# Decoder layer on one core: residual rows ahead of the copies of V on the DMA queue, and cross attention in pairs of chunks

## The reference

```python
# cross attention, 16 heads of 64 (as the kernel computes it)
e   = clip(exp(q @ k.T / sqrt(64)), exp(-11), exp(11))
o   = (e @ v) / e.sum(-1)
x   = layernorm(x + concat(o) @ Wo + bo)
# each of 6 layers: local attention, window 32, rows of two tiles of 128 tokens
qkv = shift(x) @ Wqkv            # shift: half of the columns come from the row before
o   = softmax(mask(rot(l2norm(q)) @ rot(l2norm(k)).T * 8)) @ v
x1  = x + o @ Wo
x2  = x1 + ffn(layernorm(shift(x1)))
```

## Time and profile before

| what | value |
|---|---|
| median of three runs | 2269.71 us (2268.53 to 2270.89) |
| the profiled execution | 2269.04 us, span 2267.3 us |
| TensorE, matmuls | 2108.9 us busy, 93% |
| VectorE, ScalarE, GpSimd | 81%, 73%, 73% |
| mean granted TensorE clock | 0.984 of 2.4 GHz |
| cross attention | from about 325 us to 624 us |
| window layers | from 624 us to the end |

### The profile page before, as it was taken

How to read it: one execution, slowest core, us unless ns; L and a number is a source line. 1 busy time by engine, 2 the same in 40 slices (tenths; PEclk the granted TensorE clock), 3 DMA queues, 4 the chain that set the end, 5 groups by cost and what they waited for, 6 DMA issues and landing times. The chain is left out here.

```text
span 2267.3 us, 70752 instructions
## 1 busy us (share of the span) xinstructions
PE 2108.9 (93%) x26387; PEld 1429.3 (63%) x26387; DVE 1840.3 (81%) x2681; ACT 1662.4 (73%) x3300; POOL 1653.9 (73%) x1553
## 2 busy tenths in 40 slices
PE   5898769999979999999999999999999999999995
PEld 3555436666546676766667666666666666666674
DVE  4898957777788888888888888888888888888883
ACT  5888845454367788788788878878877787887773
POOL 4667843332378888888888888888888888888881
PEclk8999989999999999999999999999999999999997
DMA  2321220000023223222322322232232222223221
GB/s 76 110 65 64 65 73 2 1 1 1 1 52 78 70 60 79 69 71 67 82 71 56 83 69 70 69 77 76 56 83 70 70 69 73 77 59 83 70 64 47
DMA packets 103501, 140.43 MB, mean 62 GB/s; under 512 B 63376, under 2 KB 64400, under 8 KB 103056
## 3 DMA queue, kind: packets, MB, share of 16 engines
q1 hardware_dynamic: 103440, 139.64, 23.1%
HBM read 56.39 MB, written 1.31 MB: 25 GB/s over the span
## 5 line engine op out<-in xcount | busy, mean ns | idle before, releaser
L1727 PE MATMUL f_psA<-f_W,f_xT 128*128 (+1 forms) x1154 | 599.4, 615 | 8.9 <-ACT f_Vt L1479 3.6
L1617 DVE TENSOR_TENSOR f_m<-f_psA,f_tab 128x1024 f32<-128x1024 f32 x385 | 458.4, 1212 | 62.9 <-ACT f_sq L1461 62.9
L1397 POOL TENSOR_TENSOR f_qkr<-f_qkr,f_rn 128x1024 f32<-128x1024 f32 x192 | 361.2, 1902 | 17.2 <-POOL f_rn L1420 17.2
L1368 POOL TENSOR_TENSOR f_Pr<-f_Pr,f_rden 128x384 f32<-128x384 f32 x384 | 307.7, 833 | 74.4 <-DVE f_rden L1606 74.4
L1461 ACT ACTIVATE f_sq<-f_psA 128x512 f32<-128x512 f32 x385 | 222.0, 589 | 103.9 <-PE f_psA L1727 100.2
L1727 PEld LDWEIGHTS f_psA<-f_W,f_xT 128*128 128x128 f32 x1154 | 191.6, 189 | 129.5 <-issue 88.4
L1387 POOL TENSOR_TENSOR f_qkr<-f_m 128x512 f32<-128x512 f32 x192 | 243.6, 1269 | 18.9 <-DVE f_m L1617 18.9
L1388 POOL TENSOR_TENSOR f_qkr<-f_m 128x512 f32<-128x512 f32 x192 | 245.6, 1279 | 0.0
L794 POOL TENSOR_TENSOR x_Es<-x_E 128x512 f32<-128x512 f32 x64 | 81.0, 1266 | 205.9 <-DVE x_E L899 205.9
L1593 DVE TENSOR_REDUCE f_mx<-f_psS 128x8 f32<-128x768 f32 x192 | 183.4, 955 | 50.0 <-PE f_psS L1762 50.0
L1648 DVE TENSOR_REDUCE f_ssq<-f_sq 128x32 f32<-128x2048 f32 x96 | 218.5, 2276 | 0.0
(11 more groups left out here) (176 smaller groups left out, 4717.1 us busy)
## 6 DMA issues: line engine op xcount, KB each, us to landing
f_V<-f_Vt SPq DMA_DIRECT2D x96, 384.0 KB, 4.2
f_V<-f_Vt SPq DMA_DIRECT2D x96, 256.0 KB, 3.5
f_W<-in_f_W SPq DMA_DIRECT2D x48, 344.0 KB, 3.0
m_Cb<-m_BC_rows SPq DMA_DIRECT2D x64, 256.0 KB, 3.1
f_W<-in_f_W SPq DMA_DIRECT2D x48, 296.5 KB, 3.5
f_V<-f_Vt SPq DMA_DIRECT2D x48, 128.0 KB, 4.3
f_xsA<-xall SPq DMA_DIRECT2D x98, 32.0 KB
f_xsA<-xall SPq DMA_DIRECT2D x98, 31.8 KB
```

Of the source, the lines that this page charges most:

```text
L1368: pool.tensor_tensor(pv, pv, rv.unsqueeze(3).broadcast_to([P, 2, 2, KEYS]), ALU.mult).then_inc(Pr_ready[g][j], 1)
L1397: pool.tensor_tensor(qv, qv, rv.unsqueeze(3).broadcast_to([P, 2, GH, DH]), ALU.mult).then_inc(qkr_ready[g], 1)
L1617: dve.tensor_tensor(m12[:, j, :, half].rearrange("p m (h d) -> p m h d", d=DH), psA[n % 2][:, :].rearrange("p (h d) -> p h d", d=DH).unsqu ...
L1727: pe.matmul(psA[n % 2][:, :], xT[:, t, :], weights(i, W_QKV + n * 512, 512), start=True, stop=True).then_inc(A_full[n_fill], 1)
```

## The change

In the window layers SyncE waits for `x1_ready` and issues the `xsC` DMAs first, and only then the copies of V. In cross attention the loop goes over pairs of chunks: each stage is run for both chunks before the next one. `E` gets four buffers (`ES`) in place of two. `out_projection` is one call that takes both row tiles of a head pair together and waits for each pair's normalised output by itself; its results go to two fills, `wo0` and `wo1`. VectorE, ScalarE and the list `fills` follow the new order.

```diff
@@ cross_attention_block, TensorE
-            for g in range(CHUNKS + 1):
+            for g in range(0, CHUNKS + 1, 2):
                 b, c = divmod(g, NC)
-                if g + 1 < CHUNKS:
-                    project(g + 1)
                 if c == 2 and b >= 1:
-                    out_projection(b - 1, 1)
+                    out_projection(b - 1)
                 if g < CHUNKS:
                     scores(g)
+                    scores(g + 1)
...
-                if g >= 1:
+                if g >= 2:
+                    times_v(g - 2)
                     times_v(g - 1)
-                if c == 1 and b >= 1:
-                    out_projection(b - 1, 0)
-                if c == 3 and b + 1 < B:
+                if g + 2 < CHUNKS:
+                    project(g + 2)
+                    project(g + 3)
+                if c == 2 and b + 1 < B:
                     transpose_rows(b + 1)
                 if c >= 4 and b + 1 < B:
                     project_v(b + 1, c - 4)
+                    project_v(b + 1, c - 3)
-            def out_projection(b, t):
...
+            def out_projection(b):
+                places = [bank(b, f"wo{t}") for t in range(TPB)]
                 for c in range(NC):
+                    pe.wait_ge(O_free, b * NC + c + 1)
+                    for t in range(TPB):
+                        ps, full = places[t]
+                        ins = pe.matmul(ps[:, 0:D], OT[:, b % 2, c, t * P:(t + 1) * P], wo[:, c, :], start=(c == 0), stop=(c == NC - 1))
...
@@ cross_attention_block, VectorE
                 if g < CHUNKS:
                     clip(g)
-                if g >= 1:
+                if g >= 2:
+                    normalise(g - 2)
+                if g < CHUNKS:
+                    clip(g + 1)
+                if g >= 2:
                     normalise(g - 1)
...
@@ window_layers, SyncE, slot(i, t, stages)
                     shift_in(i + 1, t)
-
-                    u = i * 2 + t
-                    for j in range(2):
-                        sp.wait_ge(A_free[8 + j], u + 1)
-                        alone(sp, passed)
-
-                    at_least(sp, O_free[1], u - 1)
-                    sp.dma_start(V96[WIN:KEYS, t, 0, :], Vt[0:HQ, t, :]).then_inc(V96_ready[t], 16)
-                    sp.dma_start(V96[:, t, 1, :], Vt[WIN:P, t, :]).then_inc(V96_ready[t], 16)
-                    if t == 1:
-                        sp.dma_start(V96[0:WIN, 1, 0, :], Vt[P - WIN:P, 0, :]).then_inc(V96_ready[t], 16)
                 if "C" in stages:
                     sp.wait_ge(x1_ready, i * 2 + (t - 1))
...
+                if "A" in stages:
+
+                    u = i * 2 + t
+                    for j in range(2):
+                        sp.wait_ge(A_free[8 + j], u + 1)
+                        alone(sp, passed)
...
```

More of the change, by code:

```diff
@@ L693, in cross_attention_block @@
     CHUNKS = B * NC
+    ES = 4
     LO, HI = float(np.exp(-11.0)), float(np.exp(11.0))
@@ L748, in cross_attention_block @@
         block = ctx.enter_context(nc.Block())
-        fills = [(0, "cat"), (0, "qk0")]
-        for g in range(CHUNKS + 1):
+        fills = [(0, "cat"), (0, "qk0"), (0, "qk1")]
+        for g in range(0, CHUNKS + 1, 2):
             b, c = divmod(g, NC)
-            if g + 1 < CHUNKS:
-                fills.append(((g + 1) // NC, f"qk{(g + 1) % NC}"))
+            if c == 2 and b >= 1:
+                fills += [(b - 1, f"wo{t}") for t in range(TPB)]
             if g == 0:
                 fills += [(0, f"v{n}") for n in range(4)]
-            if c == 1 and b >= 1:
-                fills.append((b - 1, "wo"))
-            if c == 3 and b + 1 < B:
+            if g + 2 < CHUNKS:
+                fills += [((g + 2) // NC, f"qk{(g + 2) % NC}"), ((g + 3) // NC, f"qk{(g + 3) % NC}")]
+            if c == 2 and b + 1 < B:
                 fills.append((b + 1, "cat"))
             if c >= 4 and b + 1 < B:
-                fills.append((b + 1, f"v{c - 4}"))
-        fills.append((B - 1, "wo"))
+                fills += [(b + 1, f"v{c - 4}"), (b + 1, f"v{c - 3}")]
+        fills += [(B - 1, f"wo{t}") for t in range(TPB)]
         place = {f: (k % 2, k // 2) for k, f in enumerate(fills)}
@@ L841, in exponentials @@
                     act.wait_ge(S_full, 2 * g + j + 1)
-                    if j == 0 and g >= 2:
-                        act.wait_ge(O_full, g - 1)
-                    act.activation(E[:, g % 2, j, :, :], psS[(2 * g + j) % 4][:, :, :], ACT.Exp, scale=DH ** -0.5).then_inc(E_exp, 1)
+                    if j == 0 and g >= ES:
+                        act.wait_ge(O_full, g - ES + 1)
+                    act.activation(E[:, g % ES, j, :, :], psS[(2 * g + j) % 4][:, :, :], ACT.Exp, scale=DH ** -0.5).then_inc(E_exp, 1)
             def copy_qk(g):
@@ L856, in _ @@
             copy_qk(0)
-            for g in range(CHUNKS + 1):
+            copy_qk(1)
+            for g in range(0, CHUNKS + 1, 2):
                 b, c = divmod(g, NC)
-                if g + 1 < CHUNKS:
-                    copy_qk(g + 1)
                 if g < CHUNKS:
                     exponentials(g)
+                    exponentials(g + 1)
                 if g == 0:
@@ L865, in _ @@
                         evacuate_v(0, n)
-                if c == 1 and b + 1 < B:
+                if g + 2 < CHUNKS:
+                    copy_qk(g + 2)
+                    copy_qk(g + 3)
+                if c == 0 and b + 1 < B:
                     deviation(b + 1)
-                if c == 3 and b >= 1:
+                if c == 2 and b + 1 < B:
+                    scale_transposed(b + 1)
+                if c == 4 and b >= 1:
                     deviation2(b - 1)
-                if c == 3 and b + 1 < B:
-                    scale_transposed(b + 1)
                 if c >= 4 and b + 1 < B:
                     evacuate_v(b + 1, c - 4)
+                    evacuate_v(b + 1, c - 3)
             deviation2(B - 1)
@@ L906, in residual @@
             def residual(b):
-                ps, free = wait_fill(dve, b, "wo")
                 dve.wait_ge(res_ready, b + 1)
-                dve.tensor_tensor(res[:, :, :], res[:, :, :], ps[:, 0:TPB * D].rearrange("p (t d) -> p t d", d=D), ALU.add).then_inc(free, 1)
+                for t in range(TPB):
+                    ps, free = wait_fill(dve, b, f"wo{t}")
+                    dve.tensor_tensor(res[:, t, :], res[:, t, :], ps[:, 0:D], ALU.add).then_inc(free, 1)
             def moments2(b):
-                wait_evacuated(dve, b, "wo")
+                for t in range(TPB):
+                    wait_evacuated(dve, b, f"wo{t}")
                 layer_norm_stats(dve, passed, mom2_ready, chain, [res[:, j, :] for j in range(TPB)], stats2, mom2)
@@ L922, in _ @@
             hats(0)
-            for g in range(CHUNKS + 1):
+            for g in range(0, CHUNKS + 1, 2):
                 b, c = divmod(g, NC)
+                if c == 2 and b + 1 < B:
+                    hats(b + 1)
                 if c == 2 and b >= 1:
@@ L1002, in times_v @@
                 ins.then_inc(O_full, 1)
-            def out_projection(b, t):
[L1005 to L1010, removed]
-                for c in range(NC):
-                    ins = pe.matmul(ps[:, t * D:(t + 1) * D], OT[:, b % 2, c, t * P:(t + 1) * P], wo[:, c, :], start=(c == 0), stop=(c == NC - 1))
-                if t == TPB - 1:
-                    ins.then_inc(full, 1)
+            def out_projection(b):
+                places = [bank(b, f"wo{t}") for t in range(TPB)]
+                for c in range(NC):
+                    pe.wait_ge(O_free, b * NC + c + 1)
+                    for t in range(TPB):
+                        ps, full = places[t]
+                        ins = pe.matmul(ps[:, 0:D], OT[:, b % 2, c, t * P:(t + 1) * P], wo[:, c, :], start=(c == 0), stop=(c == NC - 1))
+                        if c == NC - 1:
+                            ins.then_inc(full, 1)
             transpose_rows(0)
             project(0)
-            for g in range(CHUNKS + 1):
+            project(1)
+            for g in range(0, CHUNKS + 1, 2):
                 b, c = divmod(g, NC)
-                if g + 1 < CHUNKS:
-                    project(g + 1)
                 if c == 2 and b >= 1:
-                    out_projection(b - 1, 1)
+                    out_projection(b - 1)
                 if g < CHUNKS:
                     scores(g)
+                    scores(g + 1)
                 if g == 0:
@@ L1036, in _ @@
                     project_v(b + 1, c - 4)
-            out_projection(B - 1, 0)
-            out_projection(B - 1, 1)
+                    project_v(b + 1, c - 3)
+            out_projection(B - 1)
 W_QKV = 0
@@ L1314, in slot @@
                     shift_in(i + 1, t)
+                if "C" in stages:
+                    sp.wait_ge(x1_ready, i * 2 + (t - 1))
+                    sp.dma_start(xsC[:, t, 0:64], x1[:, t, 0:64]).then_inc(xsC_ready[t], 16)
+                    sp.dma_start(xsC[1:P, t, 64:D], x1[0:P - 1, t, 64:D]).then_inc(xsC_ready[t], 16)
```

(3 more changed lines are left out.)

21 lines of the change are left out of this document (7 added, 14 removed).

## The result

The changed kernel takes **2354.28 us** (median of 4 runs, 2352.89 to 2357.59) against 2269.12 us for the kernel before in the same comparison: a ratio of 1.0376, 95% interval 1.0358 to 1.0394. It is slower, as forecast, but by 85 us and not 55, and 4 us beyond the upper end of my range. The profiled execution took 2353.36 us (span 2351.6).

A forecast was written before the change was run, and what follows sets the result against it. The prediction took TensorE's instruction list, 93% busy, as the bound. From the profiled 2269.04 us it summed -4 (cross attention), -13 (order's gain) and +74 (late V) to 2326, stated as 2325 us, range 2290 to 2350.

The forecast's parts named there:

- Direction and place: Whole kernel 2.4% slower, as ScalarE waits for V's late copies from t = 1 in the window layers; chance of slower 0.87.
- the wait, 1.6 taken: Window layers: ScalarE waits 1.6 us per iteration for V's copies, all lost on TensorE: +73.6 us.
- Case 2: Window layers: the engine busy with the 127-row DMA delays V in full, 2.0 us per iteration: 2344 us; chance 0.20.
- Case 5: Window layers: V's issues held back behind three small DMAs, 0.9 us on top of Case 2: 2385 us; chance 0.07.
- The gain of the order: Window layers, t = 0: earlier residual rows cut idle time before the second `scores` by 0.29 us per iteration: -13 us.
- Cross attention: -4 forecast: Cross attention in sum: -17.6 + 4 + 7.4 + 2 = -4 us, between -12 and +2.
- the 17.6: Cross attention: each of 32 chunk pairs pays 0.55 us for changes of the array's form once, not twice: -17.6 us.
- 4 and 7.4: Cross attention, seven batches: PSUM bank waits of 0.18 us three times each, +4; 1.05 us before each `out_projection`, +7.4.
- the last batch's gain: Cross attention, last batch, where no V is projected: VectorE is tight there, so its gain from pairing was given back.
- 2 for the start and the end: Cross attention: VectorE's later last normalise and four V fills at the start waiting for four exponentials: +2 us.
- Case 3: Window layers: V's copies land in time, within 6.1 us of the end of `x1`: faster, 2252 us; chance 0.11.
- Case 4: Window layers: TensorE's lost time covers other waits, 0.8 us less per iteration: 2289 us; chance 0.07.

The follow-up runs named there:

- experiments 2 and 3: The changed kernel with the new queue order at t = 0 only: ratio 0.9947; at t = 1 only: 1.0377; with four `Vt` buffers for two: 0.9923.
- one row: The changed kernel with the 127-row residual DMA L1329 cut to a single row, the others left zero: 2337.98 us, ratio 1.0287.
- experiment 5: Three variants of the changed kernel: single-row DMA L1331 behind V's copies, ratio 1.0349; 127-row DMA cut to 112 rows, 1.0297; to a single row, 1.0287.
- 112 rows: The changed kernel with the 127-row residual DMA L1329 cut to 112 rows, the last 15 left zero: 2340.95 us, ratio 1.0297.

## Why the prediction came out as it did

- **Direction and place: right.** V's copies became the late ones, at t = 1, 43 times in the stretch; experiments 2 and 3 show that this wait and nothing else makes the loss. That TensorE loses nearly the whole of it holds: 1.92 - 0.30 = 1.62, and the period grows by 1.51.
- **The failed step is the sum's form.** I priced TensorE's idle time at its own length, once per iteration. The runs show a second price: 13 iterations in which the granted clock falls to 1.2 GHz, 1.58 us each, 21 us in all. It was in no case and in no bound of the range. Without it the time would be 2353 - 21 = 2332 us, inside the range. I had read a full clock in the earlier trace rows and taken it as a constant, though it had been read where TensorE never waited longer than 0.64 us in an iteration.
- **A term mis-sized: the wait, 1.6 taken, 1.94 measured.** I had V's first issue 2.1 us behind the end of `x1`; it stands at 2.39. Between the end of L1331's issue (1589.48 + 0.87) and L1340 there are 0.27 us and not 0.04, where SyncE's list has its waits on V. The landing adds 0.1 (4.4 against 4.3). 1.5 + 0.29 + 0.1 = 1.9. With the gain taken off, an iteration was priced at 1.31 us and grew by 1.51, 9 us over 46; this error alone, without the drops, would have left the time inside the range, and so would the drops alone without it.
- **Case 2, right in size by another cause.** Its 2.0 us is nearly what was measured, but its mechanism is not. By the rule that I drew from the Trainium skill (DMA: Bandwidth & Descriptors, section "Queues, rings and completion order") one engine's ring would delay V by 0.5 us. With one row in place of 127 V's landing stays at 4.5 us. That doesn't refute the rule: L1329 is issued at 1588.81, its engine is free 3.2 us later, at 1592.0 by the earlier trace rows, and V's data starts to move 1.2 us behind 1590.62, at 1591.8, so hardly anything overlaps. The row that landed behind all of V in experiment 5 agrees with it.
- **Case 5, issue held back: didn't come.** V's three issues took 0.49, 0.59 and 0.59 us behind the small ones. What there is of it, 0.28 us in L1331's issue, was in the sum already, which had 0.86 for it.
- **The gain of the order: right where it can be seen.** 0.57 became 0.27 as forecast, so 0.3 per iteration, and the sum above needs it.
- **Cross attention: -4 forecast, -8 measured** (the kernel with the pairs alone is 7 us faster). Seven batches bring 7 x 0.82 = 5.7. My terms for them give 4.0 (15.4 of the 17.6, less 4 and 7.4): a pair with V takes 8.40 to 8.46 us and not 8.5, and the wait ahead of the output projection is 0.9 us and not 1.05. I had given the last batch's gain back and added 2 for the start and the end; they bring some 2.5 as well.
- **The weights of the cases.** Case 3 (faster) decided at 6.1 us from the end of `x1` to the landing; it took 3.56 + 4.4 = 8.0. Case 4 (half absorbed) had nothing for it in any run.

## What to carry to other kernels

A queue that is issued in order is a schedule: before a DMA is moved ahead, ask of each one that it passes how much slack it has, and where a buffer is given back late, count a second buffer before a second order. Here two more buffers turned 3.8% slower into 0.8% faster. Where the engine that sets the pace runs at its full granted clock because it is never idle, a new wait of 1.9 us on it can cost more than its own length; put a case for the clock into the range.

## What the runs showed of the hardware

- **Short waits on a busy TensorE brought clock drops.** With one wait of 1.92 us in the mean in each iteration of 34.7, the engine 90% busy over the span, 13 of 44 iterations had a drop of 3.4 us to 1.2 GHz; with 1.7 us in the mean (112 rows, one row) 8 and 10 had one; with two waits of 1.2 to 1.3 us, none; with the wait filled by matmuls, none. The Trainium skill (TensorE: Matmul & The Clock Gate, "Part 1: The HAM clock gate") says that activity releases the throttle and names two levels. The levels agree, 0.50 and 1.00 in the rows, and the filler agrees that activity holds the clock. The drops are not scattered: in the changed kernel the long iterations start 106 or 140 us apart (at t = 1: 1412, 1517, 1657, 1797, 1937, 2043, 2148 us), every third or fourth one, and each drop begins 2.9 to 3.6 us after the start of a wait. What picks out these waits no run here shows.
- **The issue of a DMA depends on its neighbour.** L1331, one row, takes 0.87 us behind the 127 rows and 0.59 to 0.60 behind one or 112; V's first copy takes 0.63 behind the 127 rows and 0.49 behind L1331.
- **A DMA of 256 bytes behind V's copies was not quick**: 3.95 us to its use. The same row ahead of V lands 1.7 us after its issue (112 rows, one row).
